# Grouped attention in a four-layer kernel: the rotation of the projected queries is put ahead of their squares, and the copy of turned queries too

## The reference, cut to what matters

```python
h = rmsnorm(hidden, attn_norm_w)
q = (h @ q_w.T).reshape(B, S, Hq, hd)      # B 8, S 128, Hq 16, hd 128
k = (h @ k_w.T).reshape(B, S, Hkv, hd)     # Hkv 4
v = (h @ v_w.T).reshape(B, S, Hkv, hd)
q = rmsnorm(q, q_norm_w).transpose(0, 2, 1, 3)
k = rmsnorm(k, k_norm_w).transpose(0, 2, 1, 3)
q = apply_rope(q, cos, sin)                # [x1*c - x2*s, x2*c + x1*s]
k = apply_rope(k, cos, sin)
scores = jnp.einsum('bhqd,bhkd->bhqk', q, k) * scale
scores = jnp.where(causal[None, None], scores, jnp.finfo(scores.dtype).min)
attn = jnp.einsum('bhqk,bhkd->bhqd', jax.nn.softmax(scores, axis=-1), v)
hidden = hidden + attn @ o_w.T
```

## Time and profile before

| | us |
|---|---|
| median of 3 runs (lowest, highest) | 1249.13 (1247.54, 1249.91) |
| the profiled execution's own time | 1247.7 |
| its span | 1245.9 |
| loop of the grouped attention, from its first scores to the last unit's output | 860 to 1135 |
| mean granted TensorE clock, share of full speed | 0.946 |

### The profile page before, as it was taken

How to read it: one execution, slowest core, us unless ns; L and a number is a source line. 1 busy time by engine, 2 the same in 40 slices (tenths; PEclk the granted TensorE clock), 3 DMA queues, 4 the chain that set the end, 5 groups by cost and what they waited for, 6 DMA issues and landing times.

```text
span 1245.9 us, 20024 instructions
## 1 busy us (share of the span) xinstructions
PE 1064.2 (85%) x6810; PEld 804.0 (65%) x6826; DVE 712.7 (57%) x1700; ACT 505.7 (41%) x1785; POOL 320.6 (26%) x440
## 2 busy tenths in 40 slices
PE   6799898699999578879999999986879999984784
PEld 2665565499999455658887878864555666653463
DVE  5567884520222477886665656555766666665334
ACT  2255556133223155665333333333445555542111
POOL 5242422122231334541000000011222222210562
PEclk9989999599999789999999999998999999997897
DMA  6765432989897216002201111230000000001785
GB/s 188 259 195 156 151 113 87 323 314 331 329 321 263 77 52 219 2 1 63 54 4 32 34 35 35 68 103 1 1 1 9 5 5 5 5 5 35 236 253 180
DMA packets 85217, 141.72 MB, mean 114 GB/s; under 512 B 10089, under 2 KB 58489, under 8 KB 79201
## 3 DMA queue, kind: packets, MB, share of 16 engines
q1 hardware_dynamic: 71193, 116.84, 28.8%
q0 software_dynamic: 4416, 12.06, 2.9%
q10 hardware_dynamic: 9508, 11.55, 2.8%
HBM read 117.51 MB, written 22.72 MB: 113 GB/s over the span
## 4 chain that ended last, share of the span: by engine, by line
PE 52%; DVE 17%; issue 9%; DMA 8%; ACT 7%; POOL 4%; SPq 3%; ACTq 0%; another core or an unknown queue 0%; DVEq 0%; POOLq 0%
PE P L968 6%; PE P L978 6%; PE P L1965 4%; PE P L1925 4%; PE P L1916 3%; ACT big L2341 3%; PE P L2058 2%; PE P L2866 2%; DMA scr_qk<-big 2%; PE P L2064 2%; DVE big L2573 2%; PE P L2111 1%; ACT big L2309 1%; DMA big<-placed 1%; PE P L1937 1%
## 5 line engine op out<-in xcount | busy, mean ns | idle before, releaser
L139 POOL TENSOR_TENSOR lrs<-lve,mhalf 128x1 f32<-128x1 f32 x64 | 36.7, 574 | 333.5 <-DVE lve L130 303.5
L576 DVE TENSOR_REDUCE small<-P 128x2 f32<-128x512 f32 x128 | 84.8, 684 | 43.4 <-PE P L403 43.0
L1009 ACT ACTIVATE big<-P,big 128x128 f32<-128x128 f32 x184 | 52.6, 369 | 123.1 <-PE P L968 105.8
L2252 ACT ACTIVATE big<-P,small 128x128 f32<-128x128 f32 x128 | 45.3, 366 | 128.3 <-DVE small L2432 128.3
L656 ACT ACTIVATE big<-P 128x512 f32<-128x512 f32 x128 | 73.8, 599 | 53.6 <-PE P L423 46.5
L968 PE MATMUL P<-big 128*128 128x128 f32 x736 | 87.3, 277 | 0.1
L968 PEld LDWEIGHTS P<-big 128*128 128x128 f32 x736 | 85.1, 194 | 0.9 <-issue 0.4
L978 PE MATMUL P<-big 128*128 128x256 f32 x368 | 83.1, 379 | 0.0
L1111 DVE COPY big<-P 128x256 f32<-128x256 f32 x23 | 9.8, 425 | 125.2 <-PE P L978 125.2
L2571 DVE TENSOR_TENSOR big<-P,big 128x512 f32<-128x512 f32 x40 | 27.6, 690 | 86.9 <-ACT big L2309 86.7
L271 PE MATMUL P<-CT,big 128*128 128x256 f32 (+1 forms) x224 | 67.7, 431 | 7.9 <-ACT big L248 4.7
(11 more groups left out here) (387 smaller groups left out, 2525.3 us busy)
## 6 DMA issues: line engine op xcount, KB each, us to landing
big<-b_w SPq DMA_DIRECT2D x23, 1028.0 KB
big<-b_w SPq DMA_DIRECT2D x23, 1024.0 KB
big<-scr_qk SPq DMA_DIRECT2D x96, 96.0 KB
big<-keys_t SPq DMA_DIRECT2D x8, 1024.0 KB, 6.5
big<-i_wgu SPq DMA_DIRECT2D x23, 352.0 KB
keys_t<-XNT ACTq DMA_DIRECT2D x24, 256.0 KB, 2.2
big<-moe_y SPq DMA_DIRECT2D x16, 256.0 KB, 4.4
big<-i_wd SPq DMA_DIRECT2D x23, 176.0 KB
```

Source lines behind the costliest of these rows:

```text
L576: dve.tensor_reduce(negM[:, h, :], P[:, h % 2, :].rearrange("p (c s) -> p c s", c=2), AX.X, ALU.max, negate=True).then_inc(a_max, 1)
L1009: act.activation(hT[j % 2][:, f, :], P[:, 2 * (j % 2) + f // 4, f % 4 * 128:f % 4 * 128 + 128], ACT.Gelu_apprx_tanh, bias=w1x[j % 3][:, 2 ...
```

## The change

The diff has three parts. (1) `rotate_queries(m)` waits for the projection (`h_pq`) and no longer for the squares, except where `SQUARES_FIRST(m)` holds: the first three groups, and every group with m % 4 = 1. (2) For the same groups `query_squares(m)` waits for the two rotated products (`h_r1`) and no longer for the projection. (3) In ACT's loop `copy_queries(m + 2)` is put ahead of `query_squares(m + 3)`, in all units. Group m+3 with (m + 3) % 4 = 1 belongs to a pass with g = 2, where DVE has the keys to rotate first.

```diff
+        def SQUARES_FIRST(m):
+            return m < 3 or m % 4 == 1
...
             def query_squares(m):
-                act.wait_ge(h_pq, m + 1)
+                if SQUARES_FIRST(m):
+                    act.wait_ge(h_pq, m + 1)
+                else:
+                    act.wait_ge(h_r1, m + 1)
                 if m > 0:
                     act.wait_ge(h_qss, m)
...
                 first(NM + m)
                 second(NM + m)
+                if m + 2 < NM:
+                    copy_queries(m + 2)
                 if m + 3 < NM:
                     query_squares(m + 3)
-                if m + 2 < NM:
-                    copy_queries(m + 2)
...
             def rotate_queries(m):
-                dve.wait_ge(h_qss, m + 1)
+                if SQUARES_FIRST(m):
+                    dve.wait_ge(h_qss, m + 1)
+                else:
+                    dve.wait_ge(h_pq, m + 1)
                 dve.wait_ge(h_krd, 1 + max(m - 1, 0) // 4)
```

## The result

The changed kernel takes 1229.04 us (median of 4 runs, 1225.05 to 1230.1), the kernel before 1249.52 (1247.54 to 1251.33): a ratio of 0.9834, 95% interval 0.9816 to 0.9852, or 20.5 us less. 1230 was forecast.

What follows compares the result with a forecast made beforehand. The prediction took PE as near its limit, with only its holes to win. Terms 2.7 + 1.5 + 2.2 + 1.5 + 5.5 + 2.9 + 2.9 = 19.2 us gave 1230 us, range 1226 to 1239.

Steps and rivals of the forecast that it cites:

- What bounds the stage: PE's holes: PE is near its limit in a steady stretch; the change can give the sum of PE's holes, not DVE's idle time.
- four holes: PE's waits per steady sequence: 0.49 and 0.29 before turned probabilities, 1.11 before scores, 0.80 before turned keys; together 2.69 us.
- to unit 8's turned probabilities: Units 4 to 7: holes of 0.9, 1.1 and 0.7 close, less new ones of 0.7, 0.9 and 0.3; gain 1.5 us.
- to unit 29's: In unit 28 divide no longer waits behind the last rotation; turned probabilities of unit 29 come 2.9 us earlier.
- to unit 30's: PE keeps 2.4 GHz behind unit 29, so units 29 to 30 take 4.7 us, not 7.58: another 2.9.
- Part (1), rotation ahead: In three units of four, DVE's rotation starts early; copy_out, maxima and keys' rotation follow; holes of 0.49, 0.29, 0.80 close.
- Part (2), squares behind it: PE's next queries wait for squares behind the rotation; cost nothing, margin near 0.03 us; bounds 0 and 1.00 per unit.
- Part (3), the copy: Queries' copy ahead of squares lets scores at g = 1 start earlier; hole 1.11 becomes 0.11, gain 1.00 us.
- Part (4), what is late next: At g = 2 the rotation waits for later squares; a new hole of 0.73 to 0.75 us before PE's queries, once a sequence.
- The slower rival: Squares come late for PE's one bank, PE waits at queries in every unit; 1259 us at the bound, chance 0.05.
- Nothing measurable: Rival: new hole 1.4, scores' 1.00 not gained, end at half clock with its 2.9 lost; 1248 us, chance 0.03.

Runs made afterwards that it cites:

- one experiment: Changed kernel with, at g = 2, the keys' copy ahead of the squares and the rotation ahead of divide: 1213.29 us beside 1219.34, stage 235.66.
- the experiment with the old end: Changed kernel with the last query group and its pass left as before: ratio 0.9887 to the kernel before, stage 246.89 us.
- the experiment: Changed kernel with the queries' copy back behind the squares (rotation alone): ratio 0.9887 to the kernel before, sequence 31.70 us, stage 247.59 us.
- the kernel without the exception: Changed kernel with SQUARES_FIRST true only for m < 3, no longer for m % 4 = 1: ratio 0.9993 to the kernel before, stage 260.16 us.
- one of two moves: Changed kernel with only the queries' rotation ahead of DVE's divide at g = 2: 1220.89 us beside 1219.38, stage 242.32 us.
- the other: Changed kernel with only ACT's copy of the turned keys ahead of the squares at g = 2: 1223.86 us, sequence 31.07 us.
- the second group: Experiments run on one chip, three of the four on the new hole; the changed kernel there: 1219.34 us, ratio 0.9854 to the kernel before.
- the third group: Experiments run on another chip, rotation ahead of divide and no exception; the changed kernel there: 1219.38 us, ratio 0.9821 to the kernel before.

## Why the prediction was right

*What bounds the stage: PE's holes.* Right. The prediction's four holes and the small one that it left out leave a floor of 29.73, and one experiment came to 29.70.

*The terms.* In the changed kernel's trace the distances between corresponding starts give, beside the forecast:

| part | forecast | measured | from the starts |
|---|---|---|---|
| unit 0 to unit 4's second turned row | 2.7 | 3.0 | 868.05 to 909.83; 865.02 to 903.80 |
| to unit 8's turned probabilities | 1.5 | 1.7 | to 944.86; to 937.12 |
| to unit 12's | 2.2 | 2.3 | to 977.85; to 967.80 |
| to unit 16's | 1.5 | 1.5 | to 1010.50; to 998.96 |
| to unit 28's | 5.5 | 5.6 | to 1108.15; to 1090.98 |
| to unit 29's | 2.9 | 3.0 | to 1116.65; to 1096.45 |
| to unit 30's | 2.9 | 2.9 | to 1124.23; to 1101.15 |

19.2 against 20.0. Two terms hang on the clock. The last one came in full here; the experiment with the old end shows that it could have been 1.5. The second one came to 1.7 although the half clock behind unit 4's wait lasted longer than before (4.07 us for 3.50 from the second turned row to the key products): the holes gave 2.3 there where 1.5 was forecast, and the clock took 0.6 back. That these nearly cancel is luck.

*Part (1), rotation ahead.* Right: `copy_out`, maxima and keys' rotation stopped being the releasers of PE's waits in steady sequences; the rotation alone gives 14.9 us.

*Part (2), squares behind it.* Right: from the mask to the turned probabilities at g = 1 PE takes 2.85 us where its own work is 2.82, so 0.03 is lost, and the margin was as thin as forecast, since a further square shows in full.

*Part (3), the copy.* The 1.00 at g = 1 is 1.04 in the trace and 1.03 in the experiment. But the prediction costed it as if it stood by itself. It pays only behind part (1): alone it lengthens the loop through DVE.

*Part (4), what is late next.* This step failed in its cause and was right in size in part by chance. "PE's queries of the following unit need it" put the hole ahead of the queries, behind the rotation, at 0.73. It stands ahead of the scores, behind the keys' copy, at 0.98 (0.84 more than the 0.14 that was there before). I had listed what ACT does at g = 2, and left out the instruction behind the two that were swapped: the copy of the keys stood at the same place in both orders, and became the latest only because everything ahead of PE's scores had come forward. The rotation's own wait is hidden behind it: it ends 0.3 us ahead of the queries, and by itself it would have been some 0.82 by the estimate above, or 0.68 beyond those 0.14, where 0.73 was said. The walk to it was sound; that the wait which hid it costs nearly the same is luck.

*The slower rival* did not come, but the kernel without the exception shows how near its kind is: with that exception gone the change is worth nothing that the runs can tell. *Nothing measurable* has a slip in its sum: 1248 leaves out both terms of 2.9 at the end, and the clock speaks only for one. With the other kept it would be about 1245.

## What to carry to other kernels

When two engines read one buffer one after the other, give the first turn to the one that other work queues behind, here DVE's rotation and not ACT's squares. Count the holes of the bound engine from start to start, over one whole period of the loop: that gave both the gain and the floor. When waits have moved, look for all that end within a few tenths of a microsecond at the next hole, including instructions that were not touched: here one of two moves left the stage as it was, the other made it 3.3 us longer, and both together gave 6.9. And judge a reordering in the set it belongs to: in this stage the copy's move costs 10.6 us alone and gives 5.1 as the last part.

## What the runs showed of the hardware that was not expected

The kernels took 10 us more in the measurement than in the experiments, and this lies in the experts at the end: from the last output to the end of the span the changed kernel takes 113.1 us in the measurement and 103.5 and 103.6 in the experiments, while its attention stage takes 242.42, 242.52 and 242.54. The 35 us after the first expert blocks, in the measurement and in the second group, show more bytes moved (the last column, GB/s) and PE busy throughout in the latter:

```profile
1142.00:1177.00 35.00, 31.03 (x139) 22.03 (x139) 11.12 (x32) 6.72 (x22) 20.87 (x22) 0.95 0.82 252
```

```profile
1143.00:1178.00 35.00, 34.90 (x166) 25.50 (x166) 15.19 (x42) 8.57 (x29) 26.06 (x27) 1.00 0.99 302
```

The same stretch has 252 GB/s in the trace of the kernel before too, and 297 to 310 in all twelve traces of the experiments, on four chips. Why the weights came slower in the measurement was not tried; that it is the chip is not shown, since the record does not name that one.

A square of 128x128 on ACT delays the next instruction by 0.15 us without an accumulator to read and by 0.25 with one, in the trace with five squares.

In the attention stage TensorE's half clock (1.2 GHz) follows idle times of 2.64 to 2.94 us in most places, and one of 4.16, and it does not follow one of 2.18 (no exception, at unit 7). The same wait can go both ways: the 2.81 in unit 0 was followed by full clock in 13 of the 14 traces, and by the half clock in the changed kernel's of the third group:

```profile
869.86 0.66 PE L1975 MATMUL P<-idf,XN 128*128 128x128 f32 x2 [2.81 <-ACT XNT L2267]
870.32 3.14 PE L1968 MATMUL P<-big 128*128 128x256 f32 x8
```

The length differs too. Behind unit 4's wait, 2.81 or 2.94, the clock fell in all 14, and from the second turned row to the key products it took 3.41 to 4.72 us where unit 0 at full clock takes 2.42. The output products behind unit 29's wait showed 3.62 before and 3.05 with the old end. The Trainium skill (TensorE: Matmul & The Clock Gate, The HAM clock gate (the "warmup" mystery)) has the gate judge on a schedule of its own that does not follow the kernel; these traces agree. A wait of this size is to be priced with a spread of about 1.5 us, and a stage difference of up to 1.3 us between two of these kernels can be the clock behind unit 4 alone.
